# A graph-network kernel on one core: attention's logits by three bf16 products per step, and relations' message rows as two float32r parts summed by two products

## The reference, cut

```python
# x (6250, 256); 100000 edges src, dst (dst sorted), edge_type_2 in {0, 1}
h = relu(layernorm(x)); x = x + L0(h)   # in, 3 layers of mean over neighbours, out
h = relu(layernorm(x)); x = x + L1(h)   # graph attention, 8 heads of 32
h = relu(layernorm(x)); x = x + L2(h)   # 2 layers: (x + agg/deg) W.T, norm, silu
h = relu(layernorm(x)); x = x + L3(h)   # relations
# L1: xh = x @ W; a_src, a_dst of each node and head
e = leaky_relu(a_src[src] + a_dst[dst], 0.2)
e = exp(e - m[dst]); alpha = e / denom[dst]
out = segment_sum(xh[src] * alpha, dst)      # then batch norm
# L3: for each relation r
msg_r = relu(relu(x @ W_r.T + b_r) @ W_r.T + b_r)
agg = segment_sum(where(rel == r, msg_r[src]), dst)
# then LSTM gates of agg, and a small network of three layers
```

## Time and profile before

| | us |
|---|---|
| median of 3 runs | 7397.44 (7396.36 to 7401.91) |
| the profiled execution | 7437.39 |
| its span, first to last instruction | 7435.7 |
| PE busy | 6182.1 (83%) |
| DVE busy | 3412.4 (46%) |
| POOL busy | 2160.0 (29%) |
| ACT busy | 2089.8 (28%) |
| attention pass, about | 3065 to 4363 |
| relations pass, about | 6065 to 7385 |

### The profile page before, as it was taken

The page is one execution under the profiler, slowest core; times in us unless marked ns, Lnnn a source line. Parts: engine busy times, 40 slices in busy tenths (PEclk is TensorE's granted clock), DMA queues, the critical chain, the costliest instruction groups (busy, mean ns, idle before and its releaser), DMA issues.

```text
span 7435.7 us, 105646 instructions
## 1 busy us (share of the span) xinstructions
PE 6182.1 (83%) x26609; PEld 4764.7 (64%) x26610; DVE 3412.4 (46%) x9380; ACT 2089.8 (28%) x5163; POOL 2160.0 (29%) x2472
## 2 busy tenths in 40 slices
PE   5888899999999999666666668999999956776776
PEld 3444477878887777544444456788777845555555
DVE  8876676641111222466666664322233334444444
ACT  2899600000000111222222222222333321222212
POOL 2000100010001111466666631000111126666664
PEclk8977899999999999777777779999999978888878
DMA  4777877787778777544444429778866643333332
GB/s 155 254 258 271 292 274 265 270 323 275 278 287 330 262 250 260 175 128 128 127 129 129 129 74 341 277 272 310 298 229 236 231 134 101 100 100 98 100 101 73
DMA packets 612190, 1547.34 MB, mean 208 GB/s; under 512 B 74359, under 2 KB 237666, under 8 KB 611939
## 3 DMA queue, kind: packets, MB, share of 16 engines
q1 hardware_dynamic: 483795, 1169.79, 44.5%
q0 software_dynamic: 128160, 374.31, 16.5%
HBM read 1240.32 MB, written 304.41 MB: 208 GB/s over the span
## 4 chain that ended last, share of the span: by engine, by line
PE 55%; DVE 15%; issue 10%; another core or an unknown queue 8%; DMA 4%; DVEq 3%; ACT 3%; SPq 1%; ACTq 1%; POOL 0%; POOLq 0%
PE psum L1375 35%; PE psum L1222 4%; PE psum L1660 4%; DVE acc L2617 3%; PE psum L1632 3%; PE psum L1524 2%; DMA slab<-adj 2%; ACT staged L1741 2%; PE psum L1644 2%; DVE ring L2639 2%; DVE hot_j L2346 1%; PE psum L1217 1%; DVE onehot L2608 1%; PE psum L1309 1%
## 5 line engine op out<-in xcount | busy, mean ns | idle before, releaser
L1375 PE MATMUL psum<-X,slab 128*128 128x512 f32 x12495 | 3115.3, 403 | 87.5 <-DVE g_x L2426 45.4
L1375 PEld LDWEIGHTS psum<-X,slab 128*128 128x128 f32 x12495 | 2352.0, 191 | 621.2 <-DVE g_x L2426 111.5
L2617 DVE TENSOR_TENSOR acc<-acc,psum 128x264 f32 (+1 forms) x1660 | 703.3, 424 | 1115.6 <-remote 548.9
L1046 POOL DMA_DIRECT2D table<-s_tab x147 | 80.3, 546 | 1942.9 <-DVE s_tab L2100 1942.9
L1524 PE MATMUL psum<-hot_j,hot_key 128*128 128x392 bf16 x1592 | 539.3, 411 | 108.4 <-ACT psum L1730 69.9
L1566 PE MATMUL psum<-ring,onehot 128*128 128x264 f32 x840 | 338.5, 549 | 215.6 <-DVE ring L2639 213.6
L1137 POOL DMA_INDIRECT ring<-rel_table,idx_slot x420 | 417.0, 993 | 247.6 <-ACT idx_slot L1847 132.1
L1137 POOL DMA_INDIRECT ring<-gat_table,idx_slot x420 | 415.8, 990 | 250.1 <-ACT idx_slot L1847 129.0
L1524 PEld LDWEIGHTS psum<-hot_j,hot_key 128*128 128x128 bf16 x1592 | 227.6, 146 | 400.7 <-issue 364.8
L1699 ACT COPY s_hT<-psum 128x256 f32<-128x256 f32 x273 | 101.8, 373 | 1219.7 <-PE psum L1217 1219.7
L1741 ACT CAST staged<-psum 128x392 fp32r<-128x392 f32 x808 | 410.0, 507 | 110.6 <-PE psum L1524 87.5
(11 more groups left out here) (425 smaller groups left out, 8086.0 us busy)
## 6 DMA issues: line engine op xcount, KB each, us to landing
slab<-adj SPq DMA_DIRECT2D x383, 1344.0 KB, 6.3
slab<-adj SPq DMA_DIRECT2D x313, 896.0 KB, 5.6
adj<-staged SPq DMA_DIRECT2D x808, 196.0 KB, 1.9
X<-table SPq DMA_DIRECT2D x32, 1792.0 KB, 12.7
nodes<-node_rows SPq DMA_DIRECT2D x166, 320.0 KB
table<-s_tab POOLq DMA_DIRECT2D x196, 256.0 KB, 3.1
own_dram<-s_out POOLq DMA_DIRECT2D x147, 128.0 KB, 5.3
g_own<-own_dram POOLq DMA_DIRECT2D x21, 896.0 KB, 7.2
```

The lines of the kernel that those rows point to most:

```text
L1375: last = nc.tensor.matmul(sums_of(j), slab[:, slab_at(c), u, j * P:(j + 1) * P], X[:, x_at(p, d), :], start=(d == 0), stop=(d == KT - 1))
L2617: V.tensor_tensor(a, a, psum[:, bank, 0:w], ALU.add).then_inc(sem("summed"), 1)
```

## The change

**Attention.** `dst_tab` (128 x 784 float32) is split once, before the pass, into three bf16 parts that add up to it: copy, then twice cast to bf16 and subtract, then a last cast; six DVE instructions. The transposed one-hots become bf16. In each step three bf16 products accumulate where one float32 product was.

**Relations.** A message row becomes two float32r parts side by side: columns 256 to 511 hold relu of the message rounded to float32r, columns 0 to 255 what the rounding left (`rest_of`, one more DVE instruction for each 128x256). `rel_table`'s rows are 2 KB long instead of 1 KB. For each tile of s1 POOL issues two stores of 256 KB for one of 256 KB, and they wait for the rests (`s1_lo`) and not for ACT. The last seven tiles get 14 rests behind the 14 adds, and four stores instead of two. The gathers of the relations pass bring 2 KB rows, into homes laid over the old memory (`fi_ring`, `fi_nodes`, `fi_tab`, and one home over `fi_tab` and `fi_tbuf`). A step has two float32r products 128x256 that accumulate, on the float32r one-hots `fi_onehot`, where one float32 product was.

```diff
-        rel_table = dram("rel_table", (2 * NP, D))
+        rel_table = dram("rel_table", (2 * NP, 2 * D))
...
-                        to = homes[r][:, u, :] if g == GAT else homes[r][:, u, 0:D]
+                        to = homes[r][:, u, :] if g == GAT else fi_rows(r, u).bitcast(F32)
...
-                    pool.wait_ge(*ev("s1_v1", t + 2))
-                    nc.gpsimd.dma_start(rel_tiles[:, :, bass.ds(t, 1), :].rearrange("p r o c -> p (r o c)"),
-                                        s_tab[:, parity, :].bitcast(F32).rearrange("p (r c) -> p r c", r=2)).then_inc(sem(f"s1_tab{parity}"), 16)
+                    pool.wait_ge(*ev("s1_lo", t + 2))
+                    for r in range(2):
+                        nc.gpsimd.dma_start(rel_tiles[:, r, bass.ds(t, 1), :].rearrange("p o c -> p (o c)"),
+                                            message_rows(r, parity).bitcast(F32)).then_inc(sem(f"s1_tab{parity}"), 16)
...
-            pe.wait_ge(*ev("dst_tab", 1))
+            pe.wait_ge(*ev("dst_parts", 1))
...
-                    last = nc.tensor.matmul(ps_logs[r % 2][:, v, :], onehots_t[r % 2][:, v, :],
-                                            dst_tab[:, bass.ds(tiles[v], 1), :].rearrange("p t h -> p (t h)"),
-                                            start=True, stop=True)
+                    for a in range(DST_PARTS):
+                        last = nc.tensor.matmul(ps_logs[r % 2][:, v, :], onehots_t[r % 2][:, v, :],
+                                                dst_parts[a][:, bass.ds(tiles[v], 1), :].rearrange("p t h -> p (t h)"),
+                                                start=(a == 0), stop=(a == DST_PARTS - 1))
...
-                        nc.tensor.matmul(psum[:, u % GB, 0:D], onehot[:, u, :], homes[r][:, v, 0:D],
-                                         start=True, stop=True).then_inc(sem("mm"), 1)
+                        for a in range(2):
+                            last = nc.tensor.matmul(psum[:, u % GB, 0:D], fi_onehot[:, u, :], fi_rows(r, v)[:, a * D:(a + 1) * D],
+                                                    start=(a == 0), stop=(a == 1))
+                        last.then_inc(sem("mm"), 1)
...
+            once(V.tensor_copy(dst_rest, dst_tab))
+            for a in range(DST_PARTS - 1):
+                once(V.tensor_copy(dst_parts[a], dst_rest))
+                once(V.tensor_tensor(dst_rest, dst_rest, dst_parts[a], ALU.subtract))
+            V.tensor_copy(dst_parts[DST_PARTS - 1], dst_rest).then_inc(sem("dst_parts"), 1)
...
+            def rest_of(rows):
+                return V.scalar_tensor_tensor(out=rows[:, 0:D], in0=rows[:, 0:D].bitcast(F32), scalar=0.0, in1=rows[:, D:2 * D].bitcast(F32),
+                                              op0=ALU.max, op1=ALU.subtract)
...
+                for r in range(2):
+                    dve.wait_ge(*ev(f"s1_v{r}", t + 2))
+                    last = rest_of(message_rows(r, parity))
+                last.then_inc(sem("s1_lo"), 1)
```

More of the change, by code:

```diff
@@ L1201, in _ @@
             pool.sem_inc(sem("x3_all_out"), 1)
-            all_stored("s1", "tab")
-            pool.wait_ge(*ev("s1_last_out", 32))
+            for n in range(2):
+                pool.wait_ge(*ev(f"s1_tab{n}", 16 + 32 * of_parity("s1", n)))
+            pool.wait_ge(*ev("s1_last_out", 64))
             gathers(FI)
```

78 lines of the change are left out of this document (58 added, 20 removed), and 2 rows, old and new, of the table TILE_EVENTS.

## The result

| | median us | runs |
|---|---|---|
| kernel before | 7399.0 (7392.98 to 7411.5) | 9 |
| changed kernel | 7419.21 (7410.13 to 7427.96) | 9 |

The ratio is 1.0024, with a 95% interval of 1.0015 to 1.0032: slower by 11 to 24 us, about 18 (20 between the medians). The forecast was 7428, slower by 31. The sign was right and the time was in the range. That was luck in good part, as the experiments show: the largest term, +31, was nothing, and a term that had been put at nothing was +13.

A forecast was written before the change was run, and what follows sets the result against it. Gather passes run by POOL's clock: ten gathers, then a wait taken to end with the last one's landing. Terms 0+1+0+6+31-5-2 = +31 on 7397 gave 7428 us, range 7310 to 7500.

The forecast's parts named there:

- the largest term, +31: Relations gather pass: with 2 KB rows the last gather lands 0.38 us later in each of 82 turns, +31 us.
- a term that had been put at nothing: Attention logits: three bf16 products for one float32 product, covered by the wait for PE's held results, cost 0.

The follow-up runs named there:

- r10: r8's kernel with the logits by one bf16 product of 48 columns a step, the three parts added by one more DVE operation a half; 7432.21 us.
- r0: The kernel before with ACT's and PE's loaded wait values in the build stage passed through one more register operation; 7423.84 us, on a chip of the faster kind.
- r8: r0's kernel again, on a chip of the slower kind; 7458.55 us, with the shipped kernel before at 7436.24 there.

## What to carry to other kernels

An engine that is idle for a third of a loop can still lengthen it. Before work on it is costed at nothing, ask what is slow while it is idle, and test it with one run that doubles that work. Splitting one product into three narrow ones trades array time for instructions. In these passes array time was nearly free (120 us less of it in relations gave 2 to 4.5) and instructions were not. Where the parts share their stationary operand, they fit side by side into one product, as r10 did. And two profiles from different chips may differ by more than the change: compare the timed runs first, and compare stages only on one chip.

## What was not expected of the hardware

The kernel before took 7399 to 7402 us on some chips and 7436 to 7440 on others, and the difference lies almost wholly in the two gather passes (1274.6 and 1289.0 us in r0, 1296.5 and 1304.9 in r8). The dense passes between them took the same on both (1702.8 and 1702.7 us from the last gather to the next first one). Each chip stands for one job, and what differs in it is open. A few register operations more for each load of wait values in the build stage cost 22 us. A drain behind each of POOL's gathers made one gather every 3.65 us out of one every 1.25, and with it PE's held results were gone. And PE has stretches of 4 to 5 us, about one in a turn of two halves, in which its results are held and its register operations take up to 1.4 us, at a granted clock of 0.98 in the one that was looked at; their cause is open.
